# A second cross attention's row maxima, mask additions and layer statistics reordered, and a gated layer's half tile stacked, on one Trainium2 core

## What is computed

```python
x = x + xattn0(layernorm(x), ctx)        # 16 heads
x = x + diff_attn(layernorm(x))
x = x + ffn0(layernorm(x), w1, w2, w3)   # gated layer: (silu(x@w1.T) * (x@w2.T)) @ w3.T, hidden width 704
x = x + xattn1(layernorm(x), mask, ctx)  # "adapter": 32 heads of 8
x = x + attn1(layernorm(x))
x = x + experts(layernorm(x))

# xattn1, per batch: q, k, v of the 32 tokens (q, k rotated), a_k, a_v of the 257 context rows
s  = max(q @ k.T / sqrt(8) + mask, float32_min)
o  = softmax(s) @ v                                        # 32 own keys
o += tanh(gate) * softmax(q @ a_k.T / sqrt(8)) @ a_v       # 257 context keys
y  = o @ Wo
```

## Time and profile before

| | us |
|---|---|
| median of 3 runs | 3411.35 (3408.48 to 3412.41) |
| the profiled execution's own time | 3412.01 |
| its span, first to last instruction | 3410.1 |
| PE busy | 3330.4 (98%) |
| DVE, ACT, POOL busy | 2307.1, 1988.8, 1820.8 |
| mean granted TensorE clock | 0.993 of full speed |

### The profile page before, as it was taken

One profiled execution on the slowest core, in us unless ns is written; L12 is line 12 of the kernel. 1 busy time (PEld: TensorE's weight loads), 2 busy tenths in 40 slices (PEclk: granted clock), 3 DMA queues, 4 the chain that ended last, 5 costly groups with the idle time before them and its releaser, 6 DMA issues.

```text
span 3410.1 us, 102745 instructions
## 1 busy us (share of the span) xinstructions
PE 3330.4 (98%) x34664; PEld 2416.3 (71%) x34673; DVE 2307.1 (68%) x6773; ACT 1988.8 (58%) x6062; POOL 1820.8 (53%) x3705
## 2 busy tenths in 40 slices
PE   9999999999899999999999999999989999999999
PEld 7888888888666776777777777777766666666665
DVE  5677787777787647777777777777767844444443
ACT  5777777777565547777777777777765411111111
POOL 4666666666565547777777777777746400000000
PEclk9999999999999999999999999999999999999999
DMA  3111111111212231111111111111136610000000
GB/s 97 58 55 53 53 57 53 53 56 54 68 48 62 75 125 42 45 48 46 44 45 45 48 44 47 45 45 45 46 85 155 190 56 18 18 18 18 18 18 6
DMA packets 280327, 187.66 MB, mean 55 GB/s; under 512 B 117165, under 2 KB 277125, under 8 KB 280213
## 3 DMA queue, kind: packets, MB, share of 16 engines
q1 hardware_dynamic: 279925, 185.75, 19.4%
q10 hardware_dynamic: 288, 0.40, 0.1%
HBM read 145.61 MB, written 36.21 MB: 53 GB/s over the span
## 4 chain that ended last, share of the span: by engine, by line
PE 54%; DVE 4%; ACT 2%; issue 1%; DMA 1%; DVEq 0%; SPq 0%; POOL 0%; ACTq 0%; POOLq 0%
PE bank_e L2603 13%; PE bank_e L2580 6%; PE b_ps_a L978 6%; PE c_ps_a L1012 5%; PE s_ps_a L985 5%; PE a_ps_a L989 3%; PE out_ps_a L1038 3%; PE c_ps_a L989 2%; PE c_ps_a L1071 2%; ACT probs_a L1145 1%; PE b_ps_a L989 1%; PE out_ps_a L1022 1%; PE m_ps_r L2198 1%; PE c_ps_a L1050 1%; PE c_ps_a L1061 1%
## 5 line engine op out<-in xcount | busy, mean ns | idle before, releaser
L1145 ACT ACTIVATE probs_a<-s_ps_a,neg_max_a 128x257 f32<-128x257 f32 x1024 | 471.9, 474 | 114.0 <-DVE neg_max_a L1255 114.0
L1186 POOL TENSOR_SCALAR probs_a<-probs_a,gated_a 128x256 f32<-128x256 f32 x1024 | 498.7, 505 | 26.4 <-POOL gated_a L1195 26.4
L2629 ACT ACTIVATE gate_e<-bank_e 128x512 f32<-128x512 f32 x128 | 76.4, 597 | 493.1 <-PE bank_e L2603 493.0
L1255 DVE TENSOR_REDUCE neg_max_a<-s_ps_a 128x1 f32<-128x257 f32 x1024 | 361.0, 414 | 0.0
L523 POOL TENSOR_SCALAR probs_i<-probs_i,inv_sum_i 128x256 f32<-128x256 f32 x512 | 243.2, 488 | 128.3 <-DVE inv_sum_i L687 123.7
L2561 POOL TENSOR_TENSOR inv_std_e<-var_eps_e,half_e 128x4 f32<-128x4 f32 x8 | 8.1, 1009 | 567.1 <-DVE var_eps_e L2643 567.1
L2746 DVE TENSOR_TENSOR hidden_e<-gate_e,bank_e 128x512 f32<-128x512 f32 x128 | 87.3, 687 | 292.6 <-PE bank_e L2603 291.0
L507 ACT ACTIVATE probs_i<-s_ps_i,neg_max_i 128x257 f32<-128x257 f32 x512 | 235.8, 473 | 69.1 <-DVE neg_max_i L758 67.3
L366 PE MATMUL a_ps_i<-w_k_i,ctx_t_i 128*128 128x256 f32 x1024 | 253.4, 391 | 5.3 <-issue 5.3
L1012 PE MATMUL c_ps_a<-w_v_a,ctx_t_a 128*32 128x256 f32 x4096 | 247.7, 382 | 0.0
L978 PE MATMUL b_ps_a<-ctx_t_a,w_qk_a 128*128 128x256 f32 x1024 | 242.3, 379 | 0.0
(11 more groups left out here) (370 smaller groups left out, 8104.0 us busy)
## 6 DMA issues: line engine op xcount, KB each, us to landing
ctx_t_i<-in_ctx_t SPq DMA_DIRECT2D x128, 256.0 KB, 2.7
ctx_t_a<-in_ctx_t SPq DMA_DIRECT2D x128, 256.0 KB, 2.7
mask_a<-in_L_xattn_mask SPq DMA_DIRECT2D x512, 4.0 KB, 1.5
v_bd_a<-v_self_a SPq DMA_DIRECT2D x512, 8.0 KB, 1.8
x_tok_i<-in_x SPq DMA_DIRECT2D x32, 128.0 KB, 2.0
x_res_i<-in_x SPq DMA_DIRECT2D x32, 128.0 KB, 2.4
x_after<-y_tok_i SPq DMA_DIRECT2D x32, 128.0 KB, 1.7
x_tok_d<-x_after SPq DMA_DIRECT2D x32, 128.0 KB, 2.2
```

What stands on the lines that cost most here:

```text
L1145: act.activation(probs[:, t, :], s_ps[:, g, 0:K], ACT.Exp, bias=neg_max[:, t:t + 1], accum_out=row_sum[:, t:t + 1]).then_inc(exp_done, 1)
L1186: pool.tensor_scalar(probs[:, t, 0:2 * P], probs[:, t, 0:2 * P], gated[:, t:t + 1], 1.0, ALU.mult, ALU.mult).then_inc(probs_ready, 1)
L1255: dve.tensor_reduce(neg_max[:, 4 * f + g:4 * f + g + 1], s_ps[:, g, 0:K], AX.X, ALU.max, negate=True).then_inc(max_ready, 1)
```

## The change

In the adapter layer: on DVE the two steps of the own-key maximum move ahead of the keys' copy; each half's mask addition is split into four of 128x32, each just ahead of its bank's row maximum (and SP's wait counts eight additions a batch in place of two); the statistics move from the end of slot b 1 to the end of slot b 3. In slot b 1 alone PE turns half 0 into `a_ps` before `b_ps`, and ACT copies the second turned half after two of half 1's exponentials instead of after four, and takes half 0's copies in the other order. In the gated layer: DVE writes the low half of the rest into the free rows 0 to 63 of the high half's tile (`rest_low`, `h_rest`), so that PE multiplies high and low of the rest at once with 128 rows; POOL's step for the rest and DVE's clearing of those rows go, and the identity's load counts on the first input's semaphore.

```diff
             if at.live(5) and at.live(1):
-                sp.wait_ge(self_added, at.count(1, 2))
+                sp.wait_ge(self_added, at.count(1, T))
                 loads.load_mask(sp, at, 5)
...
             if at.live(1):
+                pe.wait_ge(probs_ready, at.count(1, T, 4))
+                if at.b() == 1:
+                    if at.live():
+                        pe.wait_ge(turn_read[1][1], at.count(0))
+                    turn(a_ps, 0, 1)
                 if at.live(2):
                     pe.wait_ge(k_ready, at.count(2))
                 else:
                     pe.wait_ge(turn_read[0][0], at.count(0))
-                pe.wait_ge(probs_ready, at.count(1, T, 4))
                 turn(b_ps, 0, 0)
-                if at.live():
-                    pe.wait_ge(turn_read[1][1], at.count(0))
-                turn(a_ps, 0, 1)
+                if at.b() != 1:
+                    if at.live():
+                        pe.wait_ge(turn_read[1][1], at.count(0))
+                    turn(a_ps, 0, 1)
...
             if at.live(1):
-                exps(at, 1)
+                exps(at, 1, 0, 2)
+            if at.live() and at.b() == 1:
+                act.activation(probs_t1[1][:, :], a_ps[:, :], ACT.Copy).then_inc(turn_read[1][1], 1)
+            if at.live(1):
+                exps(at, 1, 2, 4)
+            if at.live() and at.b() != 1:
+                act.activation(probs_t1[1][:, :], a_ps[:, :], ACT.Copy).then_inc(turn_read[1][1], 1)
...
             if at.live(1):
-                act.wait_ge(turned[0][0], at.count(1))
-                act.activation(probs_t0[at.b(1) % 2][0][:, :], b_ps[:, :], ACT.Copy).then_inc(turn_read[0][0], 1)
+                if at.b() == 1:
+                    copy_turned(at, 1)
+                else:
+                    copy_turned(at, 0)
                 act.wait_ge(self_ready, at.count(1))
                 act.activation(self_e[:, :, :], self_s[:, :, :], ACT.Exp).then_inc(self_exp, 1)
-                act.wait_ge(turned[0][1], at.count(1))
-                act.activation(probs_t0[at.b(1) % 2][1][:, :], a_ps[:, :], ACT.Copy).then_inc(turn_read[0][1], 1)
+                if at.b() == 1:
+                    copy_turned(at, 0)
+                else:
+                    copy_turned(at, 1)
...
         def maxima(at, f):
...
-            dve.tensor_tensor(self_s[:, 4 * f:4 * f + 4, :], s_ps[:, :, K:N], mask[at.b(1)][:, :].unsqueeze(1).broadcast_to([P, 4, L]), ALU.add).then_inc(self_added, 1)
             for g in range(4):
+                dve.tensor_tensor(self_s[:, 4 * f + g, :], s_ps[:, g, K:N], mask[at.b(1)][:, :], ALU.add).then_inc(self_added, 1)
                 dve.tensor_reduce(neg_max[:, 4 * f + g:4 * f + g + 1], s_ps[:, g, 0:K], AX.X, ALU.max, negate=True).then_inc(max_ready, 1)
...
+            if at.live(1):
+                dve.wait_ge(self_added, at.count(1, T))
+                dve.tensor_reduce(self_max[:, :], self_s[:, :, :], AX.X, ALU.max).then_inc(self_step, 1)
+                dve.wait_ge(self_step, at.count(1, 2, 1))
+                dve.tensor_scalar(self_max[:, :], self_max[:, :], -3.4028234663852886e38, None, ALU.max).then_inc(self_step, 1)
             if at.live(2):
                 dve.wait_ge(k_full, at.count(2))
                 dve.tensor_copy(k_t[at.b(2) % 2][:, :, 0:2 * P], b_ps[:, :].rearrange("p (f n) -> p f n", f=2)).then_inc(k_ready, 1)
             if at.live(1):
                 weights(at, 1)
-                dve.wait_ge(self_added, at.count(1, 2))
-                dve.tensor_reduce(self_max[:, :], self_s[:, :, :], AX.X, ALU.max).then_inc(self_step, 1)
-                dve.wait_ge(self_step, at.count(1, 2, 1))
-                dve.tensor_scalar(self_max[:, :], self_max[:, :], -3.4028234663852886e38, None, ALU.max).then_inc(self_step, 1)
...
-            if at.b() == 1 and at.live_chunk(2):
-                dve.wait_ge(x_tok_in, at.chunks(2, 16))
-                dve.bn_stats(stats[:, :], x_tok[:, :]).then_inc(ln_step, 1)
...
+            if at.b() == 3 and at.live_chunk(3):
+                statistics(at)
...
+        statistics(At(-3, 3))
         slot(At(-2, 1))
...
# gated layer: gpsimd
+                if n == PARTS:
+                    continue
                 pool.wait_ge(h_high, part(i, n))
# tensor
-                pe.wait_ge(h_low, part(i, k))
+                if k < PARTS:
+                    pe.wait_ge(h_low, i * PARTS + k + 1)
+                else:
+                    pe.wait_ge(h_rest, i + 1)
...
-                    for s in range(2):
-                        last = pe.matmul(down_ps[c][:, :], down_w[of(k), k, c * P:c * P + P], hs[s][of(k), k, :], start=k == 0 and s == 0, stop=k == PARTS and s == 1)
+                    for s in range(2 if k < PARTS else 1):
+                        last = pe.matmul(down_ps[c][:, :], down_w[:, k, c * P:c * P + P], hs[s][:, k, :], start=k == 0 and s == 0, stop=k == PARTS)
# vector
-        dve.memset(hs[0][0:REST, PARTS, :].bitcast(F32), 0.0)
...
+        def rest_low(i):
+            dve.wait_ge(h_high, part(i, PARTS))
+            if i > 0:
+                dve.wait_ge(down_full, 2 * i)
+            dve.tensor_tensor(hs[0][0:REST, PARTS, :], hidden[part(i, PARTS) % 3][REST:P, :], hs[0][REST:P, PARTS, :], ALU.subtract).then_inc(h_rest, 1)
...
+            rest_low(i)
             if ahead:
                 low_of_x(i + 1)
```

More of the change, by code:

```diff
@@ L1139, in scalar, with exps @@
         act.activation(gate[:, :], gate[:, :], ACT.Tanh).then_inc(const_ready, 1)
-        def exps(at, f):
-            for g in range(4):
+        def exps(at, f, first, end):
+            for g in range(first, end):
                 t = 4 * f + g
@@ L1145, in exps, with copy_turned @@
                 act.activation(probs[:, t, :], s_ps[:, g, 0:K], ACT.Exp, bias=neg_max[:, t:t + 1], accum_out=row_sum[:, t:t + 1]).then_inc(exp_done, 1)
+        def copy_turned(at, r):
+            act.wait_ge(turned[0][r], at.count(1))
+            act.activation(probs_t0[at.b(1) % 2][r][:, :], a_ps[:, :] if r else b_ps[:, :], ACT.Copy).then_inc(turn_read[0][r], 1)
         def slot(at):
             if at.live(1):
-                exps(at, 0)
+                exps(at, 0, 0, 4)
             if at.live():
@@ L1156, in slot @@
             if at.live(1):
-                exps(at, 1)
+                exps(at, 1, 0, 2)
[5 more added lines that the diff above has]
+                act.activation(probs_t1[1][:, :], a_ps[:, :], ACT.Copy).then_inc(turn_read[1][1], 1)
             if at.live():
-                act.activation(probs_t1[1][:, :], a_ps[:, :], ACT.Copy).then_inc(turn_read[1][1], 1)
                 act.wait_ge(self_full, at.count(0))
@@ L1248, in maxima @@
         def maxima(at, f):
+            if f == 0 and at.live():
+                dve.wait_ge(self_exp, at.count(0))
             dve.wait_ge(scores_done, at.count(1, T, 4 - 4 * f))
@@ L1278, in select, with statistics @@
                 dve.tensor_tensor(attn_t[:, :, :], attn_t[:, :, :], out_ps[:, 2 * P:4 * P].rearrange("p (f n) -> p f n", f=2), ALU.add).then_inc(out_read, 1)
+        def statistics(at):
+            dve.wait_ge(x_tok_in, at.chunks(3, 16))
+            dve.bn_stats(stats[:, :], x_tok[:, :]).then_inc(ln_step, 1)
+            dve.wait_ge(ln_step, at.chunks(3, 2, 1))
+            dve.sem_inc(waited, 1)
+            dve.bn_aggr(mean_var[:, :], stats[:, :]).then_inc(ln_step, 1)
+            dve.wait_ge(ln_step, at.chunks(3, 2))
+            dve.tensor_scalar(var_eps[:, :], mean_var[:, 1:2], 1e-5, None, ALU.add).then_inc(ln_dve, 1)
         def slot(at):
             if at.live(1):
-                if at.live():
-                    dve.wait_ge(self_exp, at.count(0))
                 maxima(at, 0)
@@ L1739, in gated_feed_forward @@
     down_ps, x_ps = bank[4:6], bank[6:8]
-    ident_in, w_in, const_ready, w_turned, w_ready = sem("ident_in"), [sem(f"w_in{k}") for k in range(3)], sem("const_ready"), sem("w_turned"), sem("w_ready")
+    w_in, const_ready, w_turned, w_ready = [sem(f"w_in{k}") for k in range(3)], sem("const_ready"), sem("w_turned"), sem("w_ready")
     x_in_sem = [sem(f"x_in{a}") for a in range(LANES)]
@@ L1744, in gated_feed_forward @@
     x_full, x_high, x_low = sem("x_full"), sem("x_high"), sem("x_low")
-    up_full, gate_ready, hidden_ready, h_high, h_low = sem("up_full"), sem("gate_ready"), sem("hidden_ready"), sem("h_high"), sem("h_low")
+    up_full, gate_ready, hidden_ready, h_high, h_low, h_rest = (
+        sem(n) for n in ("up_full", "gate_ready", "hidden_ready", "h_high", "h_low", "h_rest"))
     down_full, y_t_ready, y_full, y_ready = sem("down_full"), sem("y_t_ready"), sem("y_full"), sem("y_ready")
@@ L1761, in preload @@
             sp.dma_start(x_tok[a][:, :], x_in[a * P:a * P + P, :]).then_inc(x_in_sem[a], 16)
-        sp.dma_start(ident[:, :], io["const"][:, C_IDENT:C_IDENT + P]).then_inc(ident_in, 16)
+        sp.dma_start(ident[:, :], io["const"][:, C_IDENT:C_IDENT + P]).then_inc(x_in_sem[0], 16)
         for n in range(2):
```

16 lines of the change are left out of this document (8 added, 8 removed).

## The result

| | before | after |
|---|---|---|
| median of the runs shown with the result | 3411.88 (4 runs) | 3388.45 (3387.49 to 3390.23, 4 runs) |
| the profiled execution's own time | 3412.01 | 3389.27 |
| its span | 3410.1 | 3387.5 |
| ratio, with 95% interval | 1 | 0.9929 [0.9915, 0.9942] |
| one chunk of the adapter layer, from one q and k projection to the next | 38.94 | 38.41 |

The account below looks back on a forecast made before the run. PE, busy for 3330.4 of 3410.1 us, was taken to bound the kernel. Adapter chunks -7.8, start -1.3 and gated layer -5.8 summed to -14.9, giving 3396.4 us; forecast's own range 3390 to 3402, stated range 3382 to 3407.

Parts of the forecast that it names:

- both gaps: Adapter layer, PE: 0.29 us before the transposes in b 1 and 0.38 before the scores in b 2 both go.
- no wait for ACT's copy in b 1: Slot b 1: ACT's copy of the second turned half, behind two exponentials instead of four, is there when PE needs it.
- the wait that takes the old one's place in b 0: Slot b 0: the keys' copy comes late, so PE meets a new wait of 0.20 us.
- 22 products in 5.22 us: Gated layer: 22 products take 5.24 us a turn, 0.73 less than the 24 before; -5.8 us over 8 turns.
- nothing on `h_rest`: Gated layer: DVE's new subtraction, costing 0.65 us, is done before PE wants its result, so the down product doesn't wait.
- the start: Start of the adapter layer: statistics taken before the copy of q and k save between 0 and 1.7 us, 1.3 taken.
- The rival with additions at their full duration: Adapter layer: 32-column additions hold up successors by 0.19 us; +9.6 us, 3420.9, slower; chance 8%.
- a sum of -14.9: Whole kernel: -7.8 us adapter chunks, -1.3 start and -5.8 gated layer, against the profiled execution's 3412.0.
- the miss of 0.22: Slot b 2: the keys' copy starts at 1933.57, so PE meets a new wait of 0.22 us.
- the forecast's first rival: Adapter layer: neither new wait, in b 0 or b 2, forms; -27.9 us, 3383.4; chance 18%.
- No new waits: Adapter layer: shorter addition distance, normalized input of 0.69 us and quicker PE resumption leave no wait; 3383.4 us; chance 18%.
- The gaps only move: Adapter layer: the order costs as much as it frees, leaving gated layer and start; -7.1 us, 3404.2; chance 18%.

Follow-up runs that it names:

- e6: Changed kernel with one mask addition of 128x128 a half again in place of four of 128x32: 3381.69 us, ratio 0.9913.
- e2: Changed kernel with the statistics back at the end of slot b 1: 3405.49 us, ratio 0.9985.
- e8: Changed kernel with POOL's two copies into the key tile ahead of its product of q in slot b 2: 3396.67 us, ratio 0.9955.
- e5: Kernel before with the gated layer's part of the change alone: 3405.84 us, ratio 0.9977.
- e10: Kernel before with only the statistics moved, from the end of slot b 1 to that of b 3: 3399.19 us, ratio 0.9961.
- e7: Changed kernel with the own-key maximum behind the keys' copy in slot b 0 alone: 3379.10 us, ratio 0.9902.
- e4: Changed kernel with the own-key maximum's two steps behind the keys' copy again, in every slot: 3396.48 us, ratio 0.9949.

## Why the prediction came out so

**Right.** The additions 0.10 to 0.11 ahead of their maxima with 0.33 behind; both gaps gone, at 0.44 and 0.99; no wait for ACT's copy in b 1; the wait that takes the old one's place in b 0; 22 products in 5.22 us; nothing on `h_rest`; the start shorter by 1.5 us, read between the first keys into `b_ps` and the first scores (7.0 before, 5.5 after), where 1.3 was taken. The rival with additions at their full duration is out: the trace has 0.18 us as duration and 0.10 as distance. The Trainium skill's page "VectorE: DVE Perf Modes", section "The TRN2 errata", gives by its formula an estimated 0.19 for the duration, and the trace agrees with that; as a cost of each small tile it is twice what a successor waited. The page's advice on many small tiles is for operands in SBUF, and this addition reads one of its two from PSUM; by sign it holds here too, since e6 has four additions in one, and is faster.

**Wrong: a sum of -14.9 where -22.7 came** in the profiled execution. The step that failed is this one, on slot b 2: "the normalized input takes about 0.69 of its 0.77 before a successor can start, and the copy starts at 1933.57". It took 0.42 until its successor (1916.09 to 1916.51). With 0.27 and the half's 0.05 less, the miss of 0.22 becomes a reserve of 0.10, and no wait forms. The wait of 0.22 that was not there is worth 31 x 0.22 = 6.8 of the 7.8 us between forecast and profiled execution. That nearly all of the 7.8 is this one term is partly luck: the smaller misses below nearly cancel.

The 0.77 was no property of the instruction. POOL's product of q started beside it in every chunk before: 1932.41 in the earlier trace rows and this row of the kernel before,

```profile
1932.42 0.61 POOL L1229 TENSOR_TENSOR q_bd_a<-qk_t_a,head_scaled_a 128x256 f32<-128x256 f32 x1
```

and in the changed kernel POOL is 0.27 ahead of DVE (1916.09):

```profile
1915.82 0.61 POOL L1247 TENSOR_TENSOR q_bd_a<-qk_t_a,head_scaled_a 128x256 f32<-128x256 f32 x1
```

| run | product of q starts ahead of the normalized input by | the latter lasts | and ends behind the product's start by |
|---|---|---|---|
| e2 | -0.05 | 0.81 | 0.76 |
| e8 | -0.03 | 0.79 | 0.76 |
| before | 0.00 | 0.77 | 0.76 |
| e5 | 0.11 | 0.65 | 0.76 |
| e10 | 0.21 | 0.55 | 0.76 |
| e7 | 0.26 | 0.51 | 0.76 |
| after | 0.27 | 0.49 | 0.76 |

So it stands in 13 of the 14 traces, all but e4's: in some 390 pairs of their steady parts the end lies 0.76 to 0.77 us behind POOL's start, wherever DVE starts, except in two single pairs where DVE came 0.41 and 0.42 behind POOL and ended 0.82 and 0.83 behind its start. In those two it lasts 0.41 and 0.40, and that is also its duration alone, at the start of the adapter layer, in every run. The trace of the kernel before had it:

```profile
1263.38 0.41 DVE L1306 TENSOR_SCALAR xn_a<-x_tok_a,mean_var_a,inv_std_a 128x256 f32<-128x256 f32 x1
```

The 0.69 of the earlier trace rows, which the forecast's first rival leans on, was no such row: POOL's product had started at 1272.72, 0.07 ahead of it, and it too ends 0.76 behind that start.

So the end of this step in b 2 is set by POOL, and DVE may come to it up to 0.35 us (0.76 - 0.41) behind POOL at no cost. That is why the additions' extra 0.19 costs in b 0 and not in b 2. The forecast moved DVE's start and kept its duration. Later than that the end moves. In e4 DVE comes 0.56 behind POOL's start:

```profile
1922.01 0.52 DVE L1334 TENSOR_SCALAR xn_a<-x_tok_a,mean_var_a,inv_std_a 128x256 f32<-128x256 f32 x1
1922.02 0.19 POOL L1249 COPY k_t_a<-k_last_a 128x2 f32 x1
1922.14 0.24 POOL L1250 COPY k_t_a<-qk_t_a 128x64 f32<-128x64 f32 x1
```

There it ends 1.07 behind the product's start and lasts 0.51, some 0.1 more than alone, beside POOL's two small copies. What delays it in all these pairs was not tried apart.

The Trainium skill's page "SBUF — State Buffer", section "SBUF: two separate sides", says that VectorE in a two-port mode and GpSimd hold a shared pair of ports by turns, and that the loser blocks and does not share. The fixed end agrees with blocking. That the pair is held "for the whole instruction" by the one that starts first is not how the durations add up: 0.61 and 0.41 would make 1.02 where 0.76 stands, and in e2 and e8 DVE starts 0.05 and 0.03 ahead and it is still DVE that lasts longer, while POOL's product stays at 0.61. Here the measurement decides; which mode this DVE instruction runs in, no run shows.

The rest of the difference is small and of both signs:
- b 0: 0.20 forecast, 0.145 + 0.055 measured. The size came out right by luck: the copy was 0.05 earlier than forecast, and the 0.055 behind a wait was not in the sum.
- b 1: 0.29 forecast, 0.345 measured, by the same 0.055: 1.7 us more of gain.
- Gated layer: -5.8 forecast, -6.6 measured. The down products are as forecast; the 24 products of the first stage behind them take 0.11 less a turn, which the forecast had unchanged, all of it at the first of them, which no longer stands behind a product of 64 rows.
- Outside the changed parts the two profiled executions differ by -1.3, about -1.4 and +2.9 us, and the adapter layer's first products by +1.1, which no step of the change explains.

**The rivals.** "No new waits" was half right: one of its two waits did not form, through the normalized input as it said, though by a mechanism that it had not. Its time, 3383.4, is 5 us from the 3388.45 that came, nearer than the forecast's 8. "The gaps only move" describes e2 exactly, so it was one edit away from what ran. The rival's condition, a PE that restarts slowly, is worth 0.055 us a wait, too little to eat up the gain.

## What to carry to other kernels

Where two engines' instructions start side by side in every iteration, a duration read there belongs to the pair: look for the same instruction alone, and check whether its end stays fixed to the other's start before its duration goes into a sum. Read what a wait costs as a distance between group starts on the bound engine, against the same pair without a wait; the totals of the waits view grew here while the kernel got faster. And where an edit helps in one slot of a loop and costs in another, make it in the one slot: the small maximum belongs ahead of the copy in b 1, not in b 0, and each of e6 and e7 gave back 0.19 to 0.20 us a chunk.

## What the runs showed of the hardware, unexpected

- VectorE's normalization of 128x256 from SBUF to SBUF takes 0.41 us alone and up to 0.82 beside GpSimd's product of two SBUF tensors of 128x256; its end stands 0.76 behind the latter's start, as long as it starts no more than 0.35 behind it.
- A subtraction of 64x512 of two SBUF operands took 1.10 us on VectorE, starting 0.74 behind a GpSimd subtraction of 128x512 that took 1.30. Its duration alone is in no row here.
- Behind a group of four transposes that had to wait for the keys' copy, the next group starts 0.49 us later in place of 0.44: b 1 before, b 0 after, b 2 in e2 and e8. The first product of such a group takes 0.165 in place of 0.109, and its weight load stands 0.01 ahead of it in place of 0.11. Groups behind the scores show the same without a wait.
- Where products of 128x512 went from 128 to 64 rows of weights or back, the last ahead of the step and the first behind it were followed after 0.32 to 0.34 us, the others after 0.23 to 0.24.
- Additions of 32 columns from PSUM last 0.18 us, and their successors start 0.10 behind.
